# Attention walks over graph edges: segment resets stored in step order and loaded for two pairs at once, target scores kept whole on chip and indexed by VectorE

## What is computed

```python
def gat_layer(x, W, a_l, a_r, b, src, dst, num_nodes):
    z = (x @ W).reshape(num_nodes, heads, d)
    el = einsum('nhd,hd->nh', z, a_l); er = einsum('nhd,hd->nh', z, a_r)
    e = el[src] + er[dst]
    e = where(e > 0, e, 0.2 * e)
    m = segment_max(e, dst); ex = exp(e - m[dst]); s = segment_sum(ex, dst)
    return segment_sum(z[src] * (ex / s[dst]), dst) + b
```

## Time and profile before

| what | us |
|---|---|
| median of three runs | 4649.5 |
| the three runs | 4644.11, 4649.5, 4653.87 |
| span of the profiled execution | 5278.5 |
| plan (0 to first instruction of rows1) | 40.8 |
| walk1, from its first gather to the end of its last | 1252.7 |
| walk2, the same | 1191.7 |
| walk3, the same | 1179.0 |

### The profile page before, as it was taken

The page is one execution under the profiler, slowest core; times in us unless marked ns, Lnnn a source line. Parts: engine busy times, 40 slices in busy tenths (PEclk is TensorE's granted clock), DMA queues, the critical chain, the costliest instruction groups (busy, mean ns, idle before and its releaser), DMA issues. The chain is left out here.

```text
span 5278.5 us, 61729 instructions
## 1 busy us (share of the span) xinstructions
PE 3093.1 (59%) x11768; PEld 1898.6 (36%) x11768; DVE 1971.5 (37%) x5574; ACT 1533.2 (29%) x4863; POOL 2683.4 (51%) x2732
## 2 busy tenths in 40 slices
PE   3245555565543454455564499911666667666699
PEld 2123233333321222222233388810333333333466
DVE  4246565555523333333336712251222222223222
ACT  2122232222221222222222133310344443434233
POOL 0366666666626666666653145525666666661121
PEclk9667776767766777767775699965777777777899
DMA  5346566666623333333335266684444444442111
GB/s 152 84 97 104 107 107 109 106 110 106 107 53 97 98 95 97 99 96 97 99 87 150 76 204 218 223 234 125 118 118 122 120 122 120 123 121 60 63 57 49
DMA packets 381422, 598.24 MB, mean 113 GB/s; under 512 B 102442, under 2 KB 272078, under 8 KB 380658
## 3 DMA queue, kind: packets, MB, share of 16 engines
q0 software_dynamic: 136000, 386.29, 32.0%
q1 hardware_dynamic: 209138, 172.22, 12.1%
q10 hardware_dynamic: 36160, 38.56, 2.4%
HBM read 489.46 MB, written 107.34 MB: 113 GB/s over the span
## 5 line engine op out<-in xcount | busy, mean ns | idle before, releaser
L583 POOL DMA_INDIRECT walk_rows<-z_two_heads,walk_idx x784 | 793.6, 1012 | 523.3 <-ACT walk_idx L596 296.0
L583 POOL DMA_INDIRECT walk_rows<-z_one_head,walk_idx x784 | 762.9, 973 | 525.0 <-ACT walk_idx L596 296.7
L1874 POOL DMA_INDIRECT walk_rows<-h,walk_idx x784 | 746.7, 952 | 462.3 <-issue 234.1
L2019 PE MATMUL walk_ps_part<-walk_rows,walk_whot 128*80 128x257 f32 x1568 | 531.0, 475 | 207.1 <-issue 109.2
L730 PE MATMUL walk_ps_part<-walk_rows,walk_whot 128*80 128x257 f32 x1568 | 538.8, 492 | 1.1 <-issue 0.9
L730 PE MATMUL walk_ps_part<-walk_rows,walk_hot 128*80 128x258 f32 x1568 | 531.2, 472 | 0.2
L596 ACT ACTIVATE walk_idx<-keep_src 128x8 int32 x212 | 44.1, 208 | 1250.4 <-remote 942.6
L2019 PEld LDWEIGHTS walk_ps_part<-walk_rows,walk_whot 128*80 128x80 f32 x1568 | 263.1, 184 | 399.7 <-issue 359.3
L730 PEld LDWEIGHTS walk_ps_part<-walk_rows,walk_whot 128*80 128x80 f32 x1568 | 277.3, 193 | 184.3 <-issue 139.1
L730 PEld LDWEIGHTS walk_ps_part<-walk_rows,walk_hot 128*80 128x80 f32 x1568 | 257.2, 182 | 134.1 <-issue 75.4
L699 PE MATMUL walk_ps_row_scores<-keep_ident,walk_fmax 32*1 32x32 f32 (+1 forms) x98 | 18.6, 190 | 439.4 <-issue 234.6
(11 more groups left out here) (371 smaller groups left out, 5054.0 us busy)
## 6 DMA issues: line engine op xcount, KB each, us to landing
exp_w<-in_ffn_W SPq DMA_DIRECT2D x108, 512.0 KB
agg<-walk_window ACTq DMA_DIRECT2D x198, 80.3 KB
walk_rows<-z_two_heads,walk_idx POOLq DMA_INDIRECT x784
walk_rows<-z_one_head,walk_idx POOLq DMA_INDIRECT x784
comb_ya<-y_tokens POOLq DMA_DIRECT2D x28, 448.0 KB
walk_rows<-h,walk_idx POOLq DMA_INDIRECT x784
walk_erB<-er_two_heads SPq DMA_DIRECT2D x104, 80.0 KB
agg<-walk_window ACTq DMA_DIRECT2D x99, 80.6 KB
```

What stands on the lines that cost most here:

```text
L583: pool.indirect_dma_start(out=Z[k // 2][:, k % 2 * GROUP_TILES + t, :], out_offset=None, in_=table, in_offset=bass.IndirectOffsetOnAxis(ap ...
L1874: pool.indirect_dma_start(out=Z[k // 2][:, k % 2 * GROUP_TILES + t, :], out_offset=None, in_=table, in_offset=bass.IndirectOffsetOnAxis(ap ...
L2019: last = pe.matmul(P[k % 2][0:WIN, 0:HW], S[k % HOTS][:, t, :], Z[k // 2][:, k % 2 * GROUP_TILES + t, :], start=t == 0, stop=t == GROUP_TI ...
```

## The change

*Plan.* `dst` is no longer loaded early by SP in the order of groups. When the step tables are made (`made` at 1), POOL issues two indirect transfers of 96 rows each, which bring the targets in the order of steps (96 partitions with two steps each). DVE makes `reset` and `rr` for 192 steps in place of 98 groups, behind its copies of `dst` and `ew`, and SP stores tables that are about twice as large (192 x 8 tiles in place of 98 x 8).

*Walks.* As the resets stand in step order, SP needs no register for them: one transfer of `reset` and one of `rr` bring two pairs, in place of twelve transfers and eight register reads. Two buffers are left; SP issues the next load when `scan_maxima` of the pair before has let go (`max_ready`), in front of the node units' loads and stores. er of all nodes is loaded once in a walk into `er_all`, spread over 128 partitions by four transfers (12704 floats a partition for two heads, 6352 for one: 6.5 and 3.25 MB in all). They are issued between the first and the second load of resets, and in walk1 so ahead of the node units' weights, on the same queue. DVE waits for them once before its first `scores`. DVE reads the two first nodes of a pair into registers itself, and `targets` takes its window out of `er_all` at that place. The window's first er, which `logits` needs, is copied into a column of `er`.

```diff
@@ plan_steps, block.sync
-            sp.dma_start(dst[:, :, :], io["dst_rows"].rearrange("(p r) w -> p r w", p=GROUPS)).then_inc(loaded, 16)
...
             sp.wait_ge(made, 2)
-            sp.dma_start(dram["reset1"].rearrange("(p r) w -> p r w", p=GROUPS), reset[:, :, :]).then_inc(stored, 16)
+            rows = reset[:, :, :, :].rearrange("p j r w -> p (j r) w")
+            sp.dma_start(dram["reset1"].rearrange("(p r) w -> p r w", p=half), rows).then_inc(stored, 16)
             for h in range(2):
...
+                sp.dma_start(dram["reset2"].rearrange("(p r h) w -> p r h w", p=half, h=2)[:, :, h, :], rows).then_inc(stored, 16)
+            sp.dma_start(dram["rr"], rr[:, :, :, :, :].rearrange("p c h j r -> p (c h j r)")).then_inc(stored, 16)
             sp.wait_ge(stored, 112)
@@ plan_steps, block.gpsimd
             pool.drain().then_inc(iotas, 1)
+            pool.wait_ge(made, 1)
+            for c in range(2):
+                pool.indirect_dma_start(
+                    out=dst[:, c, :, :].rearrange("p r w -> p (r w)"), out_offset=None,
+                    in_=io["dst_rows"].rearrange("(g r) w -> g (r w)", r=per),
+                    in_offset=bass.IndirectOffsetOnAxis(ap=gi[0:half, c:c + 1], axis=0)).then_inc(rows_in, 16)
@@ plan_steps, block.vector
             dve.drain().then_inc(made, 1)
-            dve.tensor_tensor(reset[:, :, :], dst[:, :, 1:TILE + 2], dst[:, :, 0:TILE + 1], ALU.not_equal)
-            dve.drain()
-            dve.tensor_scalar(reset[:, :, :], reset[:, :, :], -BIG, None, ALU.mult)
-            dve.drain()
-            for c in range(2):
-                for h in range(2):
-                    dve.tensor_reduce(rr[:, c, h, :], reset[:, :, c:c + TILE], axis=AX.X, op=ALU.min)
-            dve.drain().then_inc(made, 1)
             dve.tensor_copy(keep["dst"][:, :], dsti[:, :])
             dve.wait_ge(cols_in, 32)
             dve.tensor_scalar(keep["ew"][:, :], keep["ew"][:, :], 0.0, None, ALU.max)
+            dve.wait_ge(rows_in, 32)
+            for j in range(2):
+                dve.tensor_tensor(reset[:, j, :, :], dst[:, j, :, 1:TILE + 2], dst[:, j, :, 0:TILE + 1], ALU.not_equal)
+            dve.drain()
+            for j in range(2):
+                dve.tensor_scalar(reset[:, j, :, :], reset[:, j, :, :], -BIG, None, ALU.mult)
+            dve.drain()
+            for c in range(2):
+                for j in range(2):
+                    dve.tensor_reduce(rr[:, c, 0, j, :], reset[:, j, :, c:c + TILE], axis=AX.X, op=ALU.min)
+            dve.drain()
+            dve.tensor_copy(rr[:, :, 1, :, :], rr[:, :, 0, :, :])
+            dve.drain().then_inc(made, 1)
             dve.wait_ge(tabs, 48)
@@ edge_walk, block.sync
-            def load(p, q):
-                sp.wait_ge(inputs_used4, p + 1)
-                sp.sem_inc(sp_tick, 1)
-                for j in range(2):
-                    g, n0 = group(sp, p * 2 + j), first_node(sp, p * 2 + j)
-                    one = bass.ds(g, 1)
...
+            def load(c, k):
+                sp.dma_start(R[k][:, :, :], dram[f"reset{H}"][bass.ds(c * (2 * ROWS), 2 * ROWS), :]
+                             .rearrange("(q r) w -> r q w", q=2)).then_inc(inputs[k], 16)
+                sp.dma_start(rr[k][:, :, :, :, :], dram["rr"][bass.ds(c * 2, 2), :]
+                             .rearrange("(o q) (c h t) -> o q c h t", o=1, c=2, h=2)[:, :, :, 0:H, :]).then_inc(inputs[k], 16)
             n = turns(sp)
-            for p in range(AHEAD + 1):
-                load(p, p % INS)
+            load(0, 0)
+            piece = NA * H // ER_LOADS
+            for k in range(ER_LOADS):
+                sp.dma_start(erA[:, k * piece:(k + 1) * piece],
+                             er_line[:, k * piece:(k + 1) * piece].to_broadcast([128, piece])).then_inc(er_in, 16)
+            load(1, 1)
             if node:
                 node.start_sp(sp)
...
                 for m in range(1, PAIRS + 1):
                     p = i * PAIRS + m
+                    if m % 2:
+                        sp.wait_ge(max_ready, p + 1)
+                        sp.sem_inc(sp_tick, 1)
+                        load(i * 2 + (m + 3) // 2, (m + 3) // 2 % 2)
                     if node:
                         node.load(sp, p, m % 2, row_of(sp, p), stored, i * (32 * PAIRS) + (32 * m - 16))
-                    load(p + AHEAD, (m + AHEAD) % INS)
-                    if node:
                         node.store(sp, p - 1, (m - 1) % 2, row_of(sp, p - 1))
@@ edge_walk, block.vector
+            def targets(n0, j, k):
                 wide = [128, GROUP_TILES, WIN]
+                if j == 0:
+                    dve.tensor_copy(er[:, :, PT], erA[:, bass.ds(n0 * H, H)])
+                window = erA[:, bass.ds(n0 * H, WIN * H)].rearrange("p (n h) -> p n h", h=H)
                 for h in range(H):
-                    dve.tensor_tensor(picked[:, :, :], S0[k % HOTS][:, :, :], erB[q][:, j, :, h].unsqueeze(1).to_broadcast(wide), ALU.mult)
+                    dve.tensor_tensor(picked[:, :, :], S0[k % HOTS][:, :, :], window[:, :, h].unsqueeze(1).to_broadcast(wide), ALU.mult)
...
             def scores(p, m, s, loaded):
-                q = m % INS
-                dve.wait_ge(inputs[q], loaded)
-                scan_el(p, q)
+                q, o = m // 2 % 2, m % 2
+                n0 = [first_node(dve, s + j) for j in range(2)]
+                if o == 0:
+                    dve.wait_ge(inputs[q], loaded)
+                scan_el(p, q, o)
...
+            dve.wait_ge(er_in, 16 * ER_LOADS)
             scores(0, 0, 0, LOADS)
```

More of the change, by code:

```diff
@@ L108, in plan_steps @@
         per = GROUP_TILES
-        dst = ph.sb("dst", [GROUPS, per, TILE + 2], I32)
-        reset = ph.sb("reset", [GROUPS, per, TILE + 1])
-        rr = ph.sb("rr", [GROUPS, 2, 2, per])
+        half = STEP_TAB // 2
+        dst = ph.sb("dst", [half, 2, per, TILE + 2], I32)
+        reset = ph.sb("reset", [half, 2, per, TILE + 1])
+        rr = ph.sb("rr", [half, 2, 2, 2, per])
         dsti = ph.sb("dsti", [128, TILES], I32)
@@ L146, in plan_steps @@
         spare, spares = ph.sb("spare", [1, MAX_UNITS // 2, 2], I32), ph.sb("spares", [1, MAX_UNITS])
-        loaded, cols_in, iotas, made, stored, tabs, nils, agg_clear = (
-            ph.sem(n) for n in ("loaded", "cols_in", "iotas", "made", "stored", "tabs", "nils", "agg_clear"))
+        loaded, cols_in, rows_in, iotas, made, stored, tabs, nils, agg_clear = (
+            ph.sem(n) for n in ("loaded", "cols_in", "rows_in", "iotas", "made", "stored", "tabs", "nils", "agg_clear"))
         idsem = ph.sem("idsem")
         block = ph.block()
-        half = STEP_TAB // 2
         @block.sync
@@ L223, in _ @@
             dve.tensor_copy(spares[:, 0:1], unitf[:, 0:1])
-            dve.wait_ge(loaded, 64)
+            dve.wait_ge(loaded, 48)
             assert WIN == 80 and NP // 16 < 1024
@@ L471, in edge_walk @@
         winx = work[:, 0:WIN]
-        INS = UNROLL // 2
-        erB = [ph.sb(f"erB{k}", [128, 2, WIN, H]) for k in range(INS)]
+        erA = ph.sb("er_all", [128, NA * H])
         picked = ph.sb("picked", [128, GROUP_TILES, WIN])
-        R = [ph.sb(f"reset{k}", [ROWS, TILE + 1]) for k in range(INS)]
-        rr = [ph.sb(f"rr{k}", [1, 2, H, 2, GROUP_TILES]) for k in range(INS)]
+        R = [ph.sb(f"reset{k}", [ROWS, 2, TILE + 1]) for k in range(2)]
+        rr = [ph.sb(f"rr{k}", [1, 2, 2, H, PT]) for k in range(2)]
         Fl = ph.sb("fmax", [ROWS, TILE])
@@ L494, in edge_walk @@
         Wp = work[:, WIN + TILE:WIN + TILE + H * CT1].rearrange("p (h t) -> p h t", h=H)
-        er = ph.sb("er", [128, H, PT])
+        er = ph.sb("er", [128, H, CT1])
         X, L = ph.sb("x", [128, 2, H, CT1]), ph.sb("l", [128, 2, H, CT1])
-        LOADS = 16 * (2 + 2 + 2)
-        inputs = [ph.sem(f"inputs{k}") for k in range(INS)]
-        (cols, inputs_used4, el_turned, ends_ready, ends_turned, ins_ready, ins_turned, max_ready, x_ready, w_ready,
+        LOADS, ER_LOADS = 16 * 2, 4
+        inputs = [ph.sem(f"inputs{k}") for k in range(2)]
+        (cols, er_in, el_turned, ends_ready, ends_turned, ins_ready, ins_turned, max_ready, x_ready, w_ready,
          sp_tick, row_tick) = (ph.sem(n) for n in (
-             "cols", "inputs_used4", "el_turned", "ends_ready", "ends_turned", "ins_ready", "ins_turned", "max_ready",
+             "cols", "er_in", "el_turned", "ends_ready", "ends_turned", "ins_ready", "ins_turned", "max_ready",
              "x_ready", "w_ready", "sp_tick", "row_tick"))
@@ L509, in edge_walk @@
         PAIRS = UNROLL // 2
-        AHEAD = 3
         def row_of(eng, v):
@@ L571, in _ @@
                 node.finish_sp(sp, [left + (n * (PAIRS // 2) + 1)] * 2)
-            for p in range(AHEAD):
-                sp.wait_ge(inputs[(1 + p) % INS], n * LOADS + LOADS)
+            for k in range(2):
+                sp.wait_ge(inputs[k], n * LOADS + LOADS)
             sp.sem_inc(sp_tick, 1)
@@ L905, in _ @@
             for m in range(PAIRS):
```

(2 more changed lines are left out.)

51 lines of the change are left out of this document (20 added, 31 removed).

## The result

The changed kernel takes 4621.2 us (median of four runs, 4620.2 to 4623.6) against 4651.6 for the kernel before: ratio 0.9942, interval 0.993 to 0.9954. It is 30 us faster. The forecast was 4647, no change, with a range from 4625: too slow by 26 us.

The account below looks back on a forecast made before the run. POOL's issuing of gathers was taken to bound both attention walks, untouched by the change. Plan +9, start of walk1 -12 and the rest 0 gave -3 us against 4649.5: 4647, no change, with a range of 4625 to 4672.

Parts of the forecast that it names:

- The step that failed: Pairs of the walks: `targets` only reads from another place, so it costs 0 and slow gathers stay.
- 47 us of slow gathers: Walk1: 784 gathers at the paused profile's mean, 0.060 us each above walk3's, add 47 us.
- The 1035 us worked out for walk1: Walk1 without pauses: undisturbed gathers at 988 us plus 47 for slow ones.
- the 1655 us: Profiled span outside the three walks' gather stretches: 5278.5 - 3623.4 = 1655 us.
- the fit of 4682 to the median: Whole kernel: 1655 us outside the walks plus 3027 of undisturbed gathers gives 4682, 0.7% from the median.
- Pauses belong to the profiled execution: Walks: 597 us of pauses are absent from timed runs; the rival that the kernel causes them, 4240 us, had 0.04.
- The starts: Plan and start of walk1: plan +9 us (+4 to +15), earlier first gather -12 (-24 to nil); together -3.
- Start of walk2: Start of walk2: `er_all` lands by 1580 at the latest, before the first scan at 1584.14, so 0.
- the wait `max_ready`: SP in the pairs, ahead of node units' load and store: gathers do not wait for it, so 0.
- the weights pass by the table: Faster rival, start of walk1: weights not held behind `er_all`, -24 us there, 4634 in all; this side given 0.24.
- the table comes slowly: Slower rival, start of walk1: `er_all` at 180 GB/s takes 36 us, +8 there, 4666 in all; chance 0.15.
- DVE as the bound: Slower rival, walks' pairs: register reads make 22.2 us a pair, 4715 at 21.5; loop fetch a few microseconds, hidden; chance 0.07.

Follow-up runs that it names:

- e7: Kernel before with an idle small copy in front of each of a pair's four products: 4612.0 us, ratio 0.9917.
- e5: Changed kernel with the window of target scores copied to PSUM once for each step: 4567.9 us, ratio 0.982.
- e6: Kernel before with the window of target scores copied to PSUM for each step: 4554.4 us, ratio 0.98.
- e8: Changed kernel with the window of target scores copied once a step to an SBUF tile at a fixed address: 4614.0 us, ratio 0.9921.
- e1: Kernel before, run again unchanged for a profile without pauses: 4647.0 us in a single run, span 4645.1.
- e2: Changed kernel with the node units' four weight loads issued first at the start of walk1: 4627.8 us, ratio 0.993.
- e9: Kernel before with the window of target scores in PSUM and the node units' weights loaded first in walk1: 4528.4 us, ratio 0.9736.
- e10: Changed kernel with weights first and 64 drains on VectorE ahead of its first wait in walk1: 4599.0 us, ratio 0.9896.

## Why the prediction was wrong, point by point

**The step that failed** is one sentence: "`targets` keeps its operations and shapes and reads from another place: 0; the slow gathers stay as they are." The operations are the same, but a product whose operand a register addresses starts 0.17 us after the sum ahead of it, not 0.08, and the third product of a pair 0.21 us after the scan ahead of it, not 0.12; and a product's start against a gather's start is what slows gathers. So the third product comes behind the gather that it held before, and walk1 has 24 us less of held time (76.5 to 52.9). That it is the start, and not the loads or the table, is shown by e7, where the old kernel with the old loads gains 37 us from idle copies, by e5 and e6, where the difference between the kernels turns round, and by e8 against e5, where the copy in SBUF brings the held gathers back. It accounts for four fifths of the gain; the 5.5 us of rows1 have no cause that a run shows. The Trainium skill (SBUF — State Buffer, section SBUF: two separate sides) states that a VectorE operation with two SBUF inputs and a GpSimd operation that reads SBUF share a port pair as an exclusive lock: whichever starts first has it for the whole instruction, and the other is blocked. The gather reads its row numbers, `walk_idx`, from SBUF. The traces agree in one direction: 488.74 ahead of 488.80 holds the gather, and with one operand in PSUM no product holds one. In the other direction they do not: the product of 734.05, begun behind the gather of 734.01, takes its usual 0.83 us beside it, as do all that begin while a gather runs (0.80 to 0.90 in every run). There the measurement decides. In all the runs with two SBUF operands the time by which a gather is held is given to within 0.1 us by the end of a product that had begun before it, but for five gathers of a walk's 784 at most.

**A size taken from a disturbed trace.** The working put 47 us of slow gathers into walk1, from means that stood in an execution with pauses. Without pauses it is 76, so there was more to win than the sum showed. The 1035 us worked out for walk1 were 26 short (1061.2 in run e1), and the 1655 us taken for all that is not a walk were 57 too many (4645.1 less the three walks is 1598). So the fit of 4682 to the median was partly luck.

**Pauses belong to the profiled execution:** right. Spans of 4645 and 4618 without any, and the changed kernel's walk2 and walk3 equal those of before.

**The starts:** right. The plan cost 11.7 for +9 (bounds 4 and 15), because the gathered targets landed at 28.9, not 25; the stores took the 14.9 us worked out. Walk1's start gave 11.3 for 12, with the weights behind the table as assumed. Their sum is +0.4 for the -3 forecast. `er_all` landed 20 us after its first issue, between the 15.3 taken and the 28 of the bound.

**Start of walk2, and the wait `max_ready`:** right, both nothing.

**The rivals at the start of walk1**, that the weights pass by the table or that the table comes slowly, did not happen. Putting the weights ahead by hand gave 15 us at that place in the changed kernel (e2) and 29 in the kernel before (e9).

**DVE as the bound:** wrong in size. The reads did not hold it (two scans of el come as near as 17.8 us), but the longer loop was refetched at each turn of walk1 behind the first two, and a stop is 8 to 11 us, not "a few microseconds". It stayed hidden in the changed kernel, where it cost 2 us, and came out as soon as the gathers got ahead (18 us in e2). The Trainium skill (Runtime: NRT & Kernel Launch, Instruction fetch mechanics) states that a taken branch to a target outside the fetched window forces a fetch before execution goes on. The five packets and the stop in each turn agree with this; that 64 idle instructions ahead of the loop remove the stop is measured in e10.

Left open: why a product with a register in its address starts 0.1 us later was not tried by itself. Where the second product of a pair holds no gather, the place of the third is not set by it, and how many such pairs a kernel has (in the changed kernel its third product still held a gather in 13 of 49) follows from nothing shown here; nor does what the first and the fourth product hold.

## What to carry to other kernels

Where GpSimd issues gathers back to back, look in the timeline for VectorE operations with two SBUF operands that run when a gather starts, and give these one operand in PSUM: it brought 95 us here, while idle copies that shift them by less than 0.1 us moved the time by up to 37, and such a shift can be taken for the edit's own merit. Before a gain is credited to a change, run the old kernel with idle instructions at the same place. Account for span against measured time first, and take sizes from an execution in which the two agree.

## What the runs showed of the hardware that was not expected

A gather of 128 rows takes 0.95 us alone and up to 1.6 when a product of two SBUF operands had begun before it, ending 0.83 us after that product; a product that begins 0.04 us behind the gather's start does not touch it, nor does the gather hold the product (0.83). A loop on VectorE that is refetched stops it for 6 to 11 us at each turn (6.4 in e8, 11.3 in e2), and 64 instructions of filler ahead of the loop end that (147 packets of instructions in e2, 102 in e10). Six and a half MB spread over 128 partitions from one row of DRAM, with 0.5 MB of weights behind them, had landed 21.6 us after the first issue (185.0 to 206.6): 7.0 MB at 325 GB/s, the latency in it.
